# Splitting one tile's attention scores into two sets of four products, in the second layer of a two-layer gated attention and expert kernel

## The chip, the cores and the metric

The kernel runs on one core of a Trainium2 chip. The metric is device time in microseconds (us), the median of several executions. The engines named below are PE (TensorE, matrix products; PEld is its loading of weights), DVE (VectorE), ACT (ScalarE), POOL (GpSimd) and SP (SyncE, which here issues DMAs). Each engine runs its own program in order; they meet by semaphores, counters that one engine raises and another waits for.

## The reference, cut to what matters

Two layers follow each other over x, 64 sequences of 64 rows of 128 numbers. Each layer is a cross attention to a context and then a layer of experts. The part that the change touches is the second layer's attention:

```
q = (query @ qw + qb)   k = (key @ kw + kb)   v = (value @ vw + vb)      # 16 heads of 8
scores = jnp.einsum('bqhd,bkhd->bhqk', q * scale, k)
attn = jax.nn.softmax(scores, axis=-1)
out = jnp.einsum('bhqk,bkhd->bqhd', attn, v)
x = x + jnp.tanh(g_xattn[1]) * (out @ out_proj_weight + out_proj_bias)
```

The second layer has no mask; the first has one. All values are 32-bit floats.

## The kernel before, in words

The 4,096 rows of x are cut into 32 tiles of 128 rows, two sequences each. The attention of both layers is one function, `attention`, called with `of(0)` and `of(1)`; `masked` is true in the first layer alone. Tiles are numbered through both layers: t runs from 0 to 31 in the first and from 32 (`NT`) to 63 in the second. Tiles are gathered in groups of two or four for the projections.

One tile's scores are 128 query rows by 16 heads by 64 keys, which fill four banks of PSUM: `S_ps[0]` holds heads 0 to 7 (half 0) and `S_ps[1]` heads 8 to 15 (half 1). `score` (line 841) writes them with eight products, for each sequence b of the tile and each quarter q of the 128 channels one. A product uses 32 rows and 64 columns of the array, at the place (q * 32, b * S) in it, so that the eight lie on eight different places. Quarters 0 and 1 write half 0, quarters 2 and 3 write half 1. In the trace each product leaves two records, so a tile has 16 (line 852).

DVE then works on each half: `maximum(h)` (line 593) takes the largest score of each row and head, `subtract(h)` (line 601) writes the scores less this maximum into `prob` in SBUF and raises `shifted`. After that the half of PSUM may be written again. PE turns the halves (`turn_probs`, line 863, into `T_ps`), ACT takes the exponential (line 530, into `probT`), and PE multiplies by the values (`attend`, line 878, into `A_ps`). There is one `S_ps` and one `T_ps`, and no second copy of either. POOL lays the keys out in blocks for the products (`k_blk`, line 427), two tiles deep.

Every engine's order is written out by hand: a list of steps, each with its items and a function that gives the time of each item, in iterations of one tile; `run` sorts by that time and, where times are equal, by the place in the list. On PE, `score` of tile t stands first in iteration t - 1, `turn_probs(1)` of tile t - 1 follows it, then `attend` of tile t - 2, the projections, `turn_probs(0)` of tile t, and at the iteration's end `turn_r` and `turn_x` for other groups. On DVE, `maximum(0)`, `subtract(0)`, `maximum(1)` and `subtract(1)` of a tile follow each other, and the smaller work (divisions, statistics, top values, slots) comes after them, ahead of the next tile's `maximum(0)`.

The semaphores that matter: `scored` counts tiles whose eight products are done, and both `maximum(0)` and `maximum(1)` wait for it. `shifted` counts subtractions, two for each tile. `score` of tile t waits for `shifted` of 2t, that is for both subtractions of tile t - 1, and for its queries (`qT_ready`, ACT line 524) and key blocks (`kblk_ready`).

Of the kernel before, what the change touches and what calls it, by code (L numbers as in the profile page):

```python
# [18 lines left out]
NT = B * S // P  # L19
# [19 lines left out]
def wait(eng, sem, value):  # L39

    if not (isinstance(value, int) and value <= 0):
        eng.wait_ge(sem, value)
# [68 lines left out]
GROUP_OF = {t: g for g in GROUPS for t in g.tiles}  # L111
# [20 lines left out]
def shift(skew):  # L132
    return lambda t: t + skew
# [21 lines left out]
def settled(skew, steady, short, later=()):  # L155
    return lambda g: g.last + (steady if g.own < short else lag(g) + skew + (g.own in later))
# [28 lines left out]
def attention(nc, ctx, space, x_all, r_xn, ws, dram, rs, hooks):  # L185
# [13 lines left out]
    def sem(name):  # L199
        return nc.alloc_semaphore(name=name)  # L200
# [65 lines left out]
    qT_ready = sem("qT_ready")  # L266
# [4 lines left out]
    zeroed = sem("zeroed")  # L271
    kblk_ready = sem("kblk_ready")
    scored = sem("scored")
    max_ready = sem("max_ready")
    shifted = sem("shifted")
    probs_turned = sem("probs_turned")
# [37 lines left out]
    def of(layer):  # L314
        w, r, hook = ws[layer], rs[layer], hooks[layer]
        masked = layer == 0
        E = E0 if masked else E1
        short = 3 if masked else LAST_GROUPS
# [270 lines left out]
        def vector(dve):  # L589
            def maximum(h):  # L590
                def step(t):
                    dve.wait_ge(scored, t + 1)
                    nc.vector.tensor_reduce(maxes[:, t % 2, h, :, :], half_of(h), X, ALU.max).then_inc(max_ready, 1)  # L593
                return step

# [171 lines left out]
        def tensor(pe):  # L767
# [59 lines left out]
            def mask_half(h, g, u):  # L827
                for k in range(2):
                    nc.tensor.matmul(S_ps[h][:, k, 0:HQ * S].rearrange("p (e k) -> p e k", k=S), w["ident_bf"][:, :],  # L829
                                     mask_bias[:, g.at(R), u, :].unsqueeze(1).to_broadcast([P, HQ, S]),  # L830
                                     start=True, stop=False, skip_group_check=True)
# [6 lines left out]
                wait(pe, shifted, 2 * t - 1)  # L838
                mask_half(0, g, t - g.first)

            def score(t):
                g = GROUP_OF[t]
                u = t - g.first
                pe.wait_ge(qT_ready, g.i + 1)
                pe.wait_ge(kblk_ready, t + 1)
                wait(pe, shifted, 2 * t)
                if masked:
                    mask_half(1, g, u)
                for b in range(2):
                    for q in range(4):  # L850
                        rows = slice(q * 32, (q + 1) * 32)
                        last = nc.tensor.matmul(S_ps[q // 2][b * S:(b + 1) * S, q % 2, 0:HQ * S], qT[rows, g.at(R), u, b * S:(b + 1) * S],  # L852
                                                k_blk[rows, t % 2, b, :, :], start=not masked, stop=True,
                                                skip_group_check=True, tile_position=(q * 32, b * S))
                last.then_inc(scored, 1)

            def turn_probs(h):
                def step(t):
# [32 lines left out]
            def output(g):  # L891
                pe.wait_ge(r["bias_ready"], 1)
                x_bank.take(y_added, g.i + 1)
                for u in range(g.n):
# [3 lines left out]
            score_ahead = (score, tiles, score_at)  # L898
            awake = [] if masked else [(lambda n: stream_into(T_ps, n), [Q // 2], lambda _, when=when: when) for when in (NT - 3.95, NT - 1.99)]
            awake += [] if masked else [(lambda n: stream_into(T_ps, n), [Q], lambda _: NT - 1)]  # L900
            steps = [score_ahead] + awake + [(turn_probs(1), tiles, shift(0)),
                     (rank if masked else rank_slots, groups, settled(7 if masked else 8, 12, short, later)), (attend, tiles, shift(1)), (logit, groups[:7], settled(6, 9, short, later)),
                     (turn_av, groups, tail(2)), (project_q, groups, head(-2)), (output, groups, tail(3)),
                     (logit, groups[7:], settled(6, 9, short, later)),
                     (project_v, late_units, unit_head(-1)), (project_k, late, head(-3)),
                     (turn_probs(0), tiles, shift(-1)), (mask_first, tiles if masked else [], shift(-2)), (turn_r, groups, settled(5, 8, short, later)), (turn_x, groups, turn_x_at)]
            run(hook["first_tensor"](pe) + steps + hook["tensor"](pe))

        main.tensor, ahead.tensor = tensor, tensor_ahead
# [966 lines left out]
```

## Time and profile before

| | us |
|---|---|
| median of 3 runs (513.63 to 516.26) | 513.66 |
| the profiled execution, whole | 512.48 |
| the profiled execution, span from first to last instruction | 510.7 |
| first layer's attention and experts | to about 280 |
| second layer's attention | about 280 to 428 |
| second layer's experts | from about 428 |

The profile is of one execution. A row of the timeline has the start from the span's beginning and the length in us, then engine, line of the kernel, operation, what is written and read, the shape, and how many instructions are merged in the row; in brackets stands how long the engine had been idle before, and who ended it. A granted clock of 1.00 is 2.4 GHz.

### The profile page before, as it was taken

What the parts mean: (1) busy time and instruction counts of PE and PEld (TensorE: products, weight loads), DVE (VectorE), ACT (ScalarE), POOL (GpSimd) and SP (SyncE); (2) the same over time, 40 slices, a digit from 0 to 9 for tenths busy, and PEclk for the clock granted to TensorE, in tenths of its full rate; (3) what the DMA queues carried; (4) which work ended last, traced back from release to release, by engine and by line L of the source; (5) the groups of instructions that cost most, each with busy time, mean ns of one, the idle gap of its engine ahead of it and who ended that gap; (6) DMA issues with size and microseconds to landing.
All of it is one profiled execution on the core that took longest, in us unless ns stands there. A gap on an engine that the chain in (4) does not pass through costs nothing.

```text
span 510.7 us, 21982 instructions
## 1 busy us (share of the span) xinstructions
PE 438.4 (86%) x8481; PEld 321.1 (63%) x8481; DVE 359.5 (70%) x949; ACT 322.7 (63%) x755; POOL 272.7 (53%) x325
## 2 busy tenths in 40 slices
PE   2788999799978785999998789998999688798986
PEld 1455677567756685999983456666667456554544
DVE  5778879878778765455541788889998787664555
ACT  2555575566766783677754556776778467676663
POOL 2632535545475268888886544544552481544444
PEclk9999999999999998899999899999999899999999
DMA  7225434232110145565436001110031000000112
GB/s 209 51 57 153 98 104 126 70 106 71 46 55 29 35 126 101 78 97 71 45 35 148 14 4 45 46 33 3 25 85 35 23 4 4 3 1 16 43 42 68
DMA packets 50629, 30.69 MB, mean 60 GB/s; under 512 B 12384, under 2 KB 46944, under 8 KB 50528
## 3 DMA queue, kind: packets, MB, share of 16 engines
q1 hardware_dynamic: 37072, 18.54, 13.6%
q0 software_dynamic: 6640, 4.67, 7.0%
q10 hardware_dynamic: 6816, 6.07, 4.2%
q8 instruction: 70, 1.15, 0.9%
q14 instruction: 31, 0.25, 0.2%
HBM read 19.41 MB, written 9.85 MB: 57 GB/s over the span
## 4 chain that ended last, share of the span: by engine, by line
PE 43%; DVE 23%; issue 18%; POOL 7%; ACT 4%; DMA 3%; ACTq 1%; DVEq 1%; POOLq 0%; SPq 0%
DVE maxes L593 8%; PE S_ps L852 6%; PE T_ps L863 5%; POOL x_mid L1145 4%; PE A_ps L878 4%; PE m_H_ps L1478 3%; DVE prob L601 3%; PE S_ps L829 2%; PE m_X_ps L1505 2%; PE Q_ps L825 2%; PE m_T_ps L1518 2%; PE f_H_ps L1197 2%; PE Q_ps L737 2%; PE m_X_ps L1489 2%; PE m_X_ps L1461 2%
## 5 line engine op out<-in xcount | busy, mean ns | idle before, releaser
L593 DVE TENSOR_REDUCE maxes<-S_ps 128x8 f32<-128x512 f32 x128 | 87.6, 685 | 40.5 <-PE S_ps L852 40.5
L427 POOL TENSOR_TENSOR k_blk<-kT,col_a 128x512 f32<-128x512 f32 x64 | 67.7, 1068 | 77.7 <-ACT kT L488 54.5
L530 ACT ACTIVATE probT<-T_ps 128x512 f32<-128x512 f32 x128 | 76.0, 594 | 43.5 <-PE T_ps L863 42.8
L863 PE MATMUL T_ps<-col_a,prob 128*128 128x128 f32 x512 | 83.4, 287 | 9.8 <-DVE prob L601 6.1
L601 DVE TENSOR_TENSOR prob<-S_ps,maxes 128x512 f32<-128x512 f32 x128 | 88.5, 692 | 4.4
L863 PEld LDWEIGHTS T_ps<-col_a,prob 128*128 128x128 f32 x512 | 56.7, 143 | 48.0 <-issue 34.4
L1145 POOL DMA_INDIRECT x_mid<-f_out,f_rows x39 | 60.9, 1562 | 11.9 <-issue 11.9
L852 PE MATMUL S_ps<-k_blk,qT 32*64 32x256 f32 x1024 | 46.5, 415 | 5.0 <-DVE prob L601 4.1
L1010 DVE TENSOR_TENSOR f_hid<-f_H_ps,f_b 128x512 f32<-128x512 f32 x39 | 27.0, 692 | 32.4 <-PE f_Y_ps L1211 27.0
L878 PE MATMUL A_ps<-v_blk,probT 128*32 128x18 f32 x4096 | 48.7, 187 | 0.2 <-issue 0.2
L878 PEld LDWEIGHTS A_ps<-v_blk,probT 128*32 128x32 f32 x4096 | 42.0, 110 | 9.7 <-issue 8.8
L1197 PE MATMUL f_H_ps<-f_rowsT,f_w_now 128*128 128x128 f32 x312 | 42.5, 280 | 4.7 <-ACT f_rowsT L1156 4.7
L1211 PE MATMUL f_Y_ps<-f_w,f_hid 128*128 x312 | 42.6, 281 | 0.7 <-ACT f_hid L1168 0.6
L1197 PEld LDWEIGHTS f_H_ps<-f_rowsT,f_w_now 128*128 128x128 f32 x312 | 39.1, 197 | 4.9 <-ACT f_rowsT L1156 4.9
L464 POOL DMA_INDIRECT sorted_rows<-r_xn,row x32 | 32.1, 1003 | 14.4 <-DVE row L673 7.0
L1211 PEld LDWEIGHTS f_Y_ps<-f_w,f_hid 128*128 128x128 f32 x312 | 38.8, 195 | 1.3 <-issue 1.1
L513 ACT ACTIVATE xn<-x_all,shift_by,rstd 128x128 f32<-128x128 f32 x64 | 31.0, 493 | 10.7 <-DVE shift_by L631 10.7
L497 ACT COPY v_blk<-Q_ps 64x256 f32<-64x256 f32 x64 | 23.9, 373 | 19.4 <-PE Q_ps L748 18.9
L1387 POOL TENSOR_SCALAR m_other<-row_constants,r_slot,r_gap 128x128 f32<-128x128 f32 x32 | 25.4, 800 | 19.7 <-DVE m_combine L1354 19.3
L449 POOL TENSOR_TENSOR x_all<-x_all,row_constants 128x512 f32<-128x512 f32 (+1 forms) x20 | 21.1, 1056 | 25.3 <-ACT xn L513 20.9
L1168 ACT ACTIVATE f_hid<-f_hid 128x512 f32<-128x512 f32 x39 | 24.6, 631 | 15.8 <-DVE f_hid L1010 15.7
L456 POOL TENSOR_SCALAR r_spread<-r_stats 128x4 f32<-128x4 f32 (+1 forms) x20 | 3.9, 194 | 55.5 <-DVE r_stats L642 55.5
(200 smaller groups left out, 867.6 us busy)
## 6 DMA issues: line engine op xcount, KB each, us to landing
f_w<-in_W ACTq DMA_DIRECT2D x16, 256.0 KB, 2.8
ctxT<-in_ctxT SPq DMA_DIRECT2D x12, 256.0 KB, 3.0
f_rows<-sorted_rows SPq DMA_DIRECT2D x39, 64.5 KB, 2.0
out<-m_final SPq DMA_DIRECT2D x32, 64.0 KB, 1.5
x_all<-in_x SPq DMA_DIRECT2D x6, 256.0 KB, 5.8
x_mid<-x_all SPq DMA_DIRECT2D x6, 256.0 KB, 2.5
x_all<-x_mid SPq DMA_DIRECT2D x6, 256.0 KB, 3.6
ctxT<-in_ctxT SPq DMA_DIRECT2D x8, 128.0 KB, 2.6
```

The source lines that it names most:

```text
L427: nc.gpsimd.tensor_tensor(k_blk[:, t % 2, :, :, :], kT[:, g.at(R), t - g.first, :].rearrange("p (b k) -> p b k", b=2).unsqueeze(2).to_broa ...
L464: pool.indirect_dma_start(r["sorted"], bass.IndirectOffsetOnAxis(ap=row[:, t:t + 1], axis=0), r_xn[:, t, :], None).then_inc(scattered[t >= ...
L513: nc.scalar.activation(xn[:, g.at(XR), u, :], x_of(t), ACT.Identity, bias=shift_by[:, g.i % NR, u:u + 1], scale=rstd[:, g.i % NR, u:u + 1] ...
L530: nc.scalar.activation(probT[:, t % 2, 4 * h:4 * h + 4, :], T_ps[:, :, :], ACT.Exp, scale=SCALE).then_inc(probT_ready, 1)
L593: nc.vector.tensor_reduce(maxes[:, t % 2, h, :, :], half_of(h), X, ALU.max).then_inc(max_ready, 1)
L601: nc.vector.tensor_tensor(prob[:, t % 2, heads, :].rearrange("p (r e) k -> p r e k", r=2), half_of(h), maxes[:, t % 2, h, :, :].unsqueeze( ...
L852: last = nc.tensor.matmul(S_ps[q // 2][b * S:(b + 1) * S, q % 2, 0:HQ * S], qT[rows, g.at(R), u, b * S:(b + 1) * S], k_blk[rows, t % 2, b, ...
L863: last = nc.tensor.transpose(T_ps[:, j, :], pair, ident[:, :])
L878: last = nc.tensor.matmul(AV[queries, m + j, :], probT[:, t % 2, j, queries], v_blk[:, g.at(R), t - g.first, c * part // S, j, :], start=T ...
L1145: pool.indirect_dma_start(r["x_mid"], bass.IndirectOffsetOnAxis(ap=rows[:, t % RINGS, D:RW].bitcast(I32), axis=0), out[:, t % DEEP, :], No ...
L1197: last = pe.matmul(H_ps[t % 2][:, n, :], w1_now[:, t % 2, n * P:(n + 1) * P], rowsT[:, t % 2, :], start=True, stop=True)
L1211: last = pe.matmul(Y_ps[t % 2][:, 0:D], hid[:, t % 2, n, :], w2[:, bass.ds(e, 1), n, :].rearrange("p a c -> p (a c)"), start=n == 0, stop= ...
```

## The change

In the second layer the eight products of a tile are made as two sets of four. The first set, quarters 0 and 1 for both sequences, fills half 0 of the scores. It is a step of its own, `score_first`, at the end of the list of iteration t - 2, which is right ahead of `score` of the same tile. It waits for queries, key blocks and `shifted` of 2t - 1, the first subtraction of the tile in front, and raises a new semaphore, `scored_first`. The second set, quarters 2 and 3, fills half 1, waits for `shifted` of 2t as all eight did, and raises `scored`. `maximum(0)` of the second layer waits for `scored_first`, `maximum(1)` still for `scored`. The first layer's products stay one set of eight.

```diff
         def vector(dve):
             def maximum(h):
                 def step(t):
-                    dve.wait_ge(scored, t + 1)
+                    if h == 0 and not masked:
+                        dve.wait_ge(scored_first, t - NT + 1)
+                    else:
+                        dve.wait_ge(scored, t + 1)
...
-            def score(t):
+            def products(t, quarters):
                 g = GROUP_OF[t]
                 u = t - g.first
-                pe.wait_ge(qT_ready, g.i + 1)
-                pe.wait_ge(kblk_ready, t + 1)
-                wait(pe, shifted, 2 * t)
-                if masked:
-                    mask_half(1, g, u)
                 for b in range(2):
-                    for q in range(4):
+                    for q in quarters:
...
-                last.then_inc(scored, 1)
+                return last
+
+            def score_first(t):
+                pe.wait_ge(qT_ready, GROUP_OF[t].i + 1)
+                pe.wait_ge(kblk_ready, t + 1)
+                pe.wait_ge(shifted, 2 * t - 1)
+                products(t, (0, 1)).then_inc(scored_first, 1)
+
+            def score(t):
+                g = GROUP_OF[t]
+                wait(pe, shifted, 2 * t)
+                if masked:
+                    pe.wait_ge(qT_ready, g.i + 1)
+                    pe.wait_ge(kblk_ready, t + 1)
+                    mask_half(1, g, t - g.first)
+                products(t, range(4) if masked else (2, 3)).then_inc(scored, 1)
...
+            split = tiles if not masked else []
+            steps = [(score_first, split[:2], score_at), score_ahead] + awake + [(turn_probs(1), tiles, shift(0)),
...
-                     (turn_probs(0), tiles, shift(-1)), (mask_first, tiles if masked else [], shift(-2)), (turn_r, groups, settled(5, 8, short, later)), (turn_x, groups, turn_x_at)]
+                     (turn_probs(0), tiles, shift(-1)), (mask_first, tiles if masked else [], shift(-2)), (turn_r, groups, settled(5, 8, short, later)), (turn_x, groups, turn_x_at), (score_first, split[2:], shift(-2))]
```

PE's order around the scores of the second layer's tile 13 (t = 45), before. `T_ps` takes the turned probabilities, `X_ps` and `Q_ps` those of other groups; the brackets name the semaphores waited for.

```order
L863 MATMUL T_ps<-col_a,prob 128x128 [waits probT_ready,shifted]
L863 MATMUL T_ps<-col_a,prob 128x128 x3
L788 MATMUL X_ps<-col_a,r_xn 128x128 [waits y_added,r_xn_ready]
L788 MATMUL X_ps<-col_a,r_xn 128x128
L852 MATMUL S_ps<-k_blk,qT 64x256 [waits shifted,kblk_ready,qT_ready]
L852 MATMUL S_ps<-k_blk,qT 64x256 x7
L863 MATMUL T_ps<-col_a,prob 128x128 [waits probT_ready,shifted]
```

The same place after the change, where lines have moved (852 is 851 now, 863 is 877, 788 is 792):

```order
L877 MATMUL T_ps<-col_a,prob 128x128 [waits probT_ready,shifted]
L877 MATMUL T_ps<-col_a,prob 128x128 x3
L792 MATMUL X_ps<-col_a,r_xn 128x128 [waits y_added,r_xn_ready]
L792 MATMUL X_ps<-col_a,r_xn 128x128
L851 MATMUL S_ps<-k_blk,qT 64x256 [waits shifted,kblk_ready,qT_ready]
L851 MATMUL S_ps<-k_blk,qT 64x256 x3
L851 MATMUL S_ps<-k_blk,qT 64x256 [waits shifted]
L851 MATMUL S_ps<-k_blk,qT 64x256 x3
L877 MATMUL T_ps<-col_a,prob 128x128 [waits probT_ready,shifted]
```

No instruction of another kind has changed its place: both sets stand where the eight products stood, and a wait stands between them. On DVE the same tile's work reads, before:

```order
L593 TENSOR_REDUCE maxes<-S_ps 128x8 [waits scored]
L601 TENSOR_TENSOR prob<-S_ps,maxes 128x512 [waits probs_turned,max_ready]
L593 TENSOR_REDUCE maxes<-S_ps 128x8 [waits scored]
L601 TENSOR_TENSOR prob<-S_ps,maxes 128x512 [waits probs_turned,max_ready]
L609 RECIPROCAL rden<-A_ps 128x32 [waits av_made]
```

and after the change:

```order
L597 TENSOR_REDUCE maxes<-S_ps 128x8 [waits scored_first]
L605 TENSOR_TENSOR prob<-S_ps,maxes 128x512 [waits probs_turned,max_ready]
L597 TENSOR_REDUCE maxes<-S_ps 128x8 [waits scored]
L605 TENSOR_TENSOR prob<-S_ps,maxes 128x512 [waits probs_turned,max_ready]
L613 RECIPROCAL rden<-A_ps 128x32 [waits av_made]
```

The order is the same; the first maximum of a tile has another semaphore to wait for.

## Rows read from the trace of the kernel before

**Rows 1.** The page: span, and busy time of each engine.

```profile
span 510.7 us, 21982 instructions
PE 438.4 (86%) x8481; PEld 321.1 (63%) x8481; DVE 359.5 (70%) x949; ACT 322.7 (63%) x755; POOL 272.7 (53%) x325
```

**Rows 2.** Windows over 280 to 428: their sum and mean of 20 us.

```profile
sum 148.00, PE 127.75 PEld 89.87 DVE 125.38 ACT 97.62 POOL 69.03; mean PE 18.25 PEld 12.84 DVE 17.91 ACT 13.95 POOL 9.86
```

**Rows 3.** Waits from 280 to 428: us in all, times, longest.

```profile
DVE maxes L593 <- PE S_ps L852: 16.8, 21, 3.0
PE S_ps L852 <- DVE prob L601: 4.1, 8, 0.8
PE T_ps L863 <- ACT probT L530: 2.3, 11, 0.3
```

**Rows 4.** Timeline around tile 13: PE reaches the scores ahead of DVE.

```profile
333.75 0.69 DVE L601 TENSOR_TENSOR prob<-S_ps,maxes 128x512 f32<-128x512 f32 x1
334.06 0.38 PE L788 MATMUL X_ps<-col_a,r_xn 128*128 128x128 f32 x2
334.55 0.27 PEld L852 LDWEIGHTS S_ps<-k_blk,qT 32*64 32x64 f32 x16 [0.35 <-issue]
334.58 0.69 PE L852 MATMUL S_ps<-k_blk,qT 32*64 32x256 f32 x16
335.37 0.69 DVE L593 TENSOR_REDUCE maxes<-S_ps 128x8 f32<-128x512 f32 x1 [0.59 <-PE S_ps L852]
```

**Rows 5.** Timeline around tile 11: PE reaches the scores behind DVE.

```profile
326.30 0.23 PEld L852 LDWEIGHTS S_ps<-k_blk,qT 32*64 32x64 f32 x16 [0.17 <-issue]
327.09 0.69 DVE L593 TENSOR_REDUCE maxes<-S_ps 128x8 f32<-128x512 f32 x1 [0.82 <-PE S_ps L852]
```

**Rows 6.** Pieces of the chain that ended last, 280 to 428: start, us, what.

```profile
290.86 0.76 PE S_ps L852 x16
...
291.65 0.70 DVE maxes L593
...
307.35 0.62 PE S_ps L852 x16
...
421.89 0.70 PE S_ps L852 x16
...
422.62 0.70 DVE maxes L593
```

**Rows 7.** Timeline around tiles 2, 5, 21 and 27: scores and the maximum behind them.

```profile
290.83 0.27 PEld L852 LDWEIGHTS S_ps<-k_blk,qT 32*64 32x64 f32 x16 [0.29 <-issue]
291.65 0.69 DVE L593 TENSOR_REDUCE maxes<-S_ps 128x8 f32<-128x512 f32 x1 [0.59 <-PE S_ps L852]
...
301.96 0.27 PEld L852 LDWEIGHTS S_ps<-k_blk,qT 32*64 32x64 f32 x16 [0.35 <-issue]
302.78 0.69 DVE L593 TENSOR_REDUCE maxes<-S_ps 128x8 f32<-128x512 f32 x1 [0.93 <-PE S_ps L852]
...
371.58 0.27 PEld L852 LDWEIGHTS S_ps<-k_blk,qT 32*64 32x64 f32 x16 [0.53 <-issue]
372.40 0.69 DVE L593 TENSOR_REDUCE maxes<-S_ps 128x8 f32<-128x512 f32 x1 [0.60 <-PE S_ps L852]
...
398.35 0.27 PEld L852 LDWEIGHTS S_ps<-k_blk,qT 32*64 32x64 f32 x16 [0.97 <-issue]
399.16 0.69 DVE L593 TENSOR_REDUCE maxes<-S_ps 128x8 f32<-128x512 f32 x1 [0.17 <-PE S_ps L852]
```

**Rows 8.** Timeline at 395: one product of 256 columns, and its reader.

```profile
395.18 0.60 PE L737 MATMUL Q_ps<-ctxT,col 128*128 128x256 f32 x2
...
395.86 0.48 ACT L488 ACTIVATE kT<-Q_ps,col 128x256 f32<-128x256 f32 x1
```

**Rows 9.** Windows, line 852, tile 13: stretch, length, PE (instructions), PEld (instructions), clock, DMA.

```profile
334.50:334.70 0.20, 0.12 (x8) 0.15 (x16) 1.00 0.00 0
334.70:334.95 0.25, 0.25 (x16) 0.12 (x15) 1.00 0.00 0
```

More of the change, by code:

```diff
@@ L273, in attention @@
     scored = sem("scored")
+    scored_first = sem("scored_first")
     max_ready = sem("max_ready")
@@ L900, in tensor @@
             awake += [] if masked else [(lambda n: stream_into(T_ps, n), [Q], lambda _: NT - 1)]
-            steps = [score_ahead] + awake + [(turn_probs(1), tiles, shift(0)),
+            split = tiles if not masked else []
+            steps = [(score_first, split[:2], score_at), score_ahead] + awake + [(turn_probs(1), tiles, shift(0)),
                      (rank if masked else rank_slots, groups, settled(7 if masked else 8, 12, short, later)), (attend, tiles, shift(1)), (logit, groups[:7], settled(6, 9, short, later)),
```

## The prediction

> **What bounds the kernel now.** The change touches the second layer's attention alone, so I read that stretch, 280 to 428, and not the page's shares [rows 1], which mix it with the first layer and the experts. The windows come first: of its 148 us PE is busy 127.75 and DVE 125.38, the other engines far less [rows 2]. No single engine is the bound; two nearly full engines hand one tile's scores to and fro. The list of waits says where: DVE's longest wait is for the scores, 16.8 us in 21 pieces, and in the other direction PE waits 4.1 us in 8 pieces, ahead of the scores, for DVE's subtraction [rows 3].
>
> Then the timeline. At tile 13 [rows 4] DVE ends its second subtraction at 334.44 (333.75 + 0.69). PE's last work before the scores begins at 334.06, and then its weight loading stands idle for 0.35 us: it waits for that subtraction. The products begin at 334.58, and the next maximum at 335.37, 0.79 us later. DVE has filled a part of this with smaller work and waits 0.59 us. Tile 11 is the other kind [rows 5]: its weight loading is idle for only 0.17 us, which is what going over to these products costs with nothing to wait for, and DVE waits 0.82 us because PE is late. The change can start work earlier at a tile of the first kind alone.
>
> Last, the chain that ended last tells what a wait is worth. Between 280 and 428 it goes from a tile's scores to the maximum behind them 11 times, first at 290.86 and last at 421.89 [rows 6]. Other waits for scores lie beside the chain: there PE's own row of products, or DVE's smaller work, is as long, and shortening them moves nothing. At five of the 11 PE was ahead of DVE: 290.86, 301.99, 334.58, 371.62 and 398.38. At the other six it came late or waited for queries, which the first set waits for too.
>
> **The change, part by part.** Nothing is added in products or DVE work, and no instruction changes its place on any engine; a wait and a semaphore's raise stand between the two sets.
>
> *The first set's earlier start.* It waits only for the first subtraction of the tile in front, which `turn_probs(0)`, just ahead of it, has waited for already. So it starts when PE arrives. How much earlier that is, I take from the idle time of the weight loading less the 0.17 us of a late tile [rows 5]: 0.29 - 0.17 = 0.12 at tile 2, 0.18 at tile 5, 0.36 at tile 21, 0.80 at tile 27 [rows 7], 0.18 at tile 13 [rows 4]. DVE can use no more than it waits: 0.59, 0.93, 0.60, 0.17 and 0.59 us. The lesser of the two is 0.12 + 0.18 + 0.36 + 0.17 + 0.18 = 1.01 us. Gains at waits beside the chain I count as nothing. The cover is what makes them worthless: PE's products and DVE's small work run on without a pause there. If that cover went, each would be worth as much as those counted, so the whole 2.88 us of DVE's five waits is the bound above for this term (PE arrives earlier too once DVE has run ahead), and nothing the bound below.
>
> *A set of four against one of eight.* The first maximum starts when four products are done instead of eight. How long four take, no row shows. The bound above is eight: 0.79 us from the first product to the maximum [rows 4]. The bound below is a single product of the same 256 columns, whose reader starts 395.86 - 395.18 = 0.68 us after it [rows 8]; this is an estimate, since the reader is ACT. So the gain lies between 0 and 0.11 us. I take 0.04, nearer to eight, since the eight run beside each other: eight records start by 334.70 and all 16 by 334.95 [rows 9], and both of a product's records have to pass in a set of four as well. At the chain's 11 passages this gives 11 x 0.04 = 0.44 us, with bounds of 0 and 1.21.
>
> A rule of the Trainium skill prices the same thing from the other end ("TensorE: Matmul & The Clock Gate", Part 3, "The cost: per-tile semaphore tail"): the tail behind tiled products grows by 4.7 ns for each tile. Four tiles fewer would be 0.02 us, an estimate from that page, and the sum would be 0.22 us less than mine.
>
> *The second set.* It waits for the second subtraction as all eight did. Where PE is early it starts when the eight started; where PE is late it stands right behind the first set with its wait already met. I cost it at nothing: the products lie on eight places of the array, and PE has all 16 weight loads started by 334.70 [rows 9]. DVE does not meet it, as it needs half 1 only after a maximum and a subtraction, 0.69 us each [rows 4]. Behind the waiting set on PE stand `turn_probs(1)` of the tile in front, `attend` and the projections; they waited behind the eight in the same way. The cost if the two sets do not run beside each other is the third rival.
>
> *The extra wait and raise.* A tile's scores begin with no more idle time than 0.17 us though they wait for three semaphores [rows 5], so a met wait shows no cost of its own. I take 0; the bound above is 0.02 us for each of the 32 tiles, as between the end of the scores at 291.62 (290.86 + 0.76) and the maximum at 291.65 in the chain [rows 6], 0.6 us in all.
>
> *Sum.* 1.01 + 0.44 = 1.45 us less. The profiled execution took 512.48 us, 1.8 more than its span [rows 1], and becomes 511.0. The median of the runs, 513.66, is 1.2 us above the profiled one; the change does not touch that difference, so the forecast is 513.66 - 1.45 = **512.2 us**. With the bounds: 513.66 - 2.88 - 1.21 = 509.6 and 513.66 + 0.6 = 514.3.
>
> **What is late next.** At tiles where DVE no longer waits, PE's own row of products sets the pace, with `turn_probs(1)` behind `T_ps`: PE waits there for ACT's exponential, 2.3 us in 11 pieces [rows 3]. DVE running ahead does not free `T_ps` sooner.
>
> **The rivals.**
>
> 1. *Nothing arrives at the end.* DVE's time goes into another wait: PE is busy 127.75 of 148 us as its pipelined ends are drawn [rows 2], and the wait of `turn_probs(1)` for ACT stays [rows 3]. For it: only 4.1 us of PE's time in the whole stretch is spent on the wait that the change relaxes. Against it: the five passages are on the chain. The time would be from 0.8 us below the present to 0.5 above, 512.9 to 514.2, around 513.5.
>
> 2. *DVE gets all its waits back.* Once DVE is ahead, the subtractions come earlier, PE starts earlier in turn, and the five waits of the chain vanish whole, with sets of four as short as one product: 2.88 + 1.21 = 4.1 us, 509.6. Half of the way beyond my sum is 2.8 us, 510.9. For it: DVE's waits of 0.59 to 0.93 us are larger than PE's spare time that I counted. Against it: six of the 11 passages have PE late, where only the smaller set helps.
>
> 3. *Slower: the second set runs behind the first.* Of a tile's 16 records eight start between 334.58 and 334.70, and the other eight between 334.70 and 334.95 [rows 4, 9]: two waves, the second 0.12 to 0.37 us behind the first. If the waves are a rule of order, so that nothing of the second set starts before the first set's second wave has, late scores take a wave or two more, some 0.25 us (the middle of the two). The chain runs from PE's earlier work into late scores nine times, first at 307.35 and last at 421.89 [rows 6]: 9 x 0.25 = 2.25 us more, against 1.01 us of gain at early tiles, gives 514.9. If it costs that at all 24 of the 32 tiles at which no wait for the subtraction is listed (8 pieces, [rows 3]), it is 6.0 us more and 518.6. It decides from 0.11 us for a late tile, where nine times that eats the gain. For it: the first set takes quarters 0 and 1 for both sequences, so its third product lies on the same rows as its first, where the eight ran through four quarters before they came back to one. Against it: all 16 weight loads had started by 334.70, among them those of products on rows that were still busy.
>
> A rule of the Trainium skill stands behind this rival ("TensorE: Matmul & The Clock Gate", Part 3, "The mechanism"): products start and end strictly in program order, and a weight load overlaps a running product only when its row group differs. By it the new order within a set would lose overlap, and the time would be that of this rival, 514.9 to 518.6. This case's trace does not bear out its second half, as 16 loads [rows 9] start while the first products of the same rows are under way.
>
> **How the numbers follow.** The forecast, 0.8 to 2.5 us less, gets 0.54; nothing at the end 0.22; all waits back 0.14; the second set behind the first 0.10. The predicted time is that of the first. The range, 510.2 to 515.4, takes in the first two cases, half of the third and the cheapest of the fourth. A change of 0.5%, 2.6 us, is about what a measurement of this kernel can tell from none. Faster by more needs 511.1 or less: the third case and the tail of the first, 0.19. Slower by more needs 516.2 or more: the dearer part of the third rival and a little for what I don't see, 0.08. The rest, 0.73, is within.
>
> **What the changed profile would show.** DVE's wait for scores should fall from 16.8 us to about 12, by more than the kernel gains, since waits beside the chain fall too. At early tiles the first records of the scores should stand right behind `turn_x`, `turn_r` or `turn_probs(0)` and ahead of the subtraction's end, and the maximum right behind DVE's smaller work. At late tiles the 16 records should still begin within 0.3 us or so; if they spread over 0.5 us or more, the third rival holds. From a set's first product to its maximum should lie about 0.75 us. I would be wrong if PE's idle time moves to `T_ps` in full, if late scores grow, or if the experts' stage behind 428 changes its length.

## The result, and the profile after

The changed kernel takes 508.97 us in the median of 20 runs (504.47 to 514.95), the kernel before 513.66 us beside it: a ratio of 0.9896, 95% interval 0.9872 to 0.9920. The medians differ by 4.7 us; the ratio leaves out the runs more than 1.5% above the fastest of their kernel (three of the changed, two of the one before), and by it the change takes 5.3 us or 1.04%, where 1.45 us were forecast. The time is outside the range given, which began at 510.2. In a second measurement the ratio was 0.9916. The profiled execution took 508.26 us, 4.22 us less than that of before.

The page of the changed kernel, with the span and the busy times, answers to [rows 1]:

```profile
span 506.5 us, 21982 instructions
PE 441.6 (87%) x8481; PEld 322.8 (64%) x8481; DVE 359.2 (71%) x949; ACT 323.1 (64%) x755; POOL 273.0 (54%) x325
```

Its windows over 280 to 428, and its waits in that stretch, answer to [rows 2, 3]:

```profile
sum 148.00, PE 131.96 PEld 93.05 DVE 126.54 ACT 100.10 POOL 69.43; mean PE 131.96 PEld 93.05 DVE 126.54 ACT 100.10 POOL 69.43
```

```profile
DVE maxes L597 <- PE S_ps L851: 14.2, 15, 2.5
...
PE T_ps L877 <- DVE prob L605: 5.0, 4, 2.9
...
PE T_ps L877 <- ACT probT L531: 2.5, 11, 0.4
...
PEld S_ps L851 <- DVE prob L605: 2.1, 4, 0.5
```

DVE's wait for scores fell from 16.8 us in 21 pieces to 14.2 in 15, by less than the forecast fall to about 12. PE's wait for the subtraction ahead of the scores is no longer among its own rows. The wait for ACT's exponential stayed (2.3 before, 2.5 now).

The timeline around tile 13, PE and DVE's maximum, answers to [rows 4]:

```profile
331.80 0.69 DVE L605 TENSOR_TENSOR prob<-S_ps,maxes 128x512 f32<-128x512 f32 x1
...
332.12 0.38 PE L792 MATMUL X_ps<-col_a,r_xn 128*128 128x128 f32 x2
...
332.43 0.33 PEld L851 LDWEIGHTS S_ps<-k_blk,qT 32*64 32x64 f32 x16 [0.17 <-issue]
332.43 0.78 PE L851 MATMUL S_ps<-k_blk,qT 32*64 32x256 f32 x16
...
333.16 0.69 DVE L597 TENSOR_REDUCE maxes<-S_ps 128x8 f32<-128x512 f32 x1 [0.32 <-PE S_ps L851]
```

The first set starts at 332.43, ahead of the end of the second subtraction (331.80 + 0.69 = 332.49), with the bare 0.17 us of going over in place of 0.35. The maximum follows 0.73 us behind the first product (0.79 before), and DVE waits 0.32 us in place of 0.59. This is what the prediction described.

Where the 4.22 us between the two profiled executions lie, by the starts of the scores in each trace (tiles are counted from 0 in each layer):

| stretch | before, us | changed, us | difference |
|---|---|---|---|
| start to tile 2 of the first layer | 25.41 | 27.02 | +1.61 |
| first layer, tiles 2 to 31 | 142.00 | 137.86 | -4.14 |
| to tile 1 of the second layer (experts between) | 119.32 | 119.42 | +0.10 |
| tiles 1 to 2 of the second layer | 4.14 | 5.11 | +0.97 |
| second layer, tiles 2 to 31 | 130.96 | 128.17 | -2.79 |
| the rest (second experts) | 88.85 | 88.88 | +0.03 |

The first and fourth rows vary as much between two traces of the changed kernel (27.02 and 25.34, 5.11 and 3.76 us), so I read nothing out of them. The surprise is the second row: the first layer's eight products were not split, and this stretch lost more than the second layer's.

Its place is found in PE's timeline. The kernel before, on its router's products and what follows:

```profile
96.70 0.74 PE L878 MATMUL A_ps<-v_blk,probT 128*32 128x18 f32 x64
97.30 0.42 PE L798 MATMUL X_ps<-col_b,r_xnT 128*32 128x8 f32 x29
99.66 0.23 PE L798 MATMUL X_ps<-col_b,r_xnT 128*32 128x8 f32 x3 [1.94 <-issue]
...
102.56 1.16 PE L852 MATMUL S_ps<-k_blk,qT 32*64 32x256 f32 x16
```

The same instructions of the changed kernel:

```profile
97.90 0.74 PE L892 MATMUL A_ps<-v_blk,probT 128*32 128x18 f32 x64
98.50 0.55 PE L802 MATMUL X_ps<-col_b,r_xnT 128*32 128x8 f32 x32
...
101.05 0.69 PE L851 MATMUL S_ps<-k_blk,qT 32*64 32x256 f32 x16
```

Before, 29 of 32 equal products run, PE stands still for 1.94 us with no semaphore to wait for ("issue"), and three follow. Windows of the kernel before show the pause and what follows it (the last three columns are the granted clock, the DMA share and GB/s):

```profile
97.70:99.60 1.90, 0.02 (x1) 0.00 (x0) 1.83 (x5) 0.00 (x0) 1.81 (x2) 1.00 0.11 35
...
101.00:103.00 2.00, 2.00 (x17) 1.41 (x23) 0.00 (x0) 1.67 (x4) 1.57 (x2) 0.54 0.66 193
103.00:105.00 2.00, 2.00 (x60) 1.06 (x46) 1.14 (x2) 0.46 (x2) 0.00 (x0) 0.61 0.76 211
```

PE had been idle, and between 101 and 105 us it runs at 0.54 and 0.61, near the lower of its two levels (1.2 of 2.4 GHz): 16 records of scores take 1.16 us in place of 0.69. In the changed kernel the clock is 1.00 there. Two more traces, of `before_again` and `layer2_order`, have a pause of 2.2 us at this place, and both have 3.4 us at the low clock behind it. From tile 17 to tile 19 of the first layer the kernel before needs 7.07 + 5.09 us, the changed one 4.36 + 4.20: 3.60 of the 4.14 us. The second layer has a pause of the same kind at 356.12 (1.18 us, the same line) in the kernel before; from the scores of that tile to the next it takes 5.25 us against 4.03 in the changed kernel.

### The profile page after: what moved, and what is told of

Its sections match the earlier page's. It is cut to its first block, busy times and chain, and to the rows that moved or that the text cites. A ratio compares the mean times of both kernels' runs of the same rounds, so it can differ in the third digit from the quotient of the medians.

```text
span 506.5 us, 21982 instructions
## 1 busy us (share of the span) xinstructions
PE 441.6 (87%) x8481; PEld 322.8 (64%) x8481; DVE 359.2 (71%) x949; ACT 323.1 (64%) x755; POOL 273.0 (54%) x325
## 3 DMA queue, kind: packets, MB, share of 16 engines
q8 instruction: 70, 1.15, 0.9%
## 4 chain that ended last, share of the span: by engine, by line
PE 46%; DVE 20%; issue 17%; ACT 6%; POOL 5%; DMA 4%; ACTq 1%; DVEq 1%; SPq 0%; POOLq 0%
DVE maxes L597 7%; PE T_ps L877 7%; PE S_ps L851 5%; PE A_ps L892 4%; PE m_H_ps L1493 3%; PE S_ps L833 2%; PE Q_ps L752 2%; POOL x_mid L1160 2%; DVE prob L605 2%; PE Q_ps L829 2%; PE m_X_ps L1520 2%; PE f_H_ps L1212 2%; PE m_T_ps L1533 2%; PE Q_ps L741 2%; DMA x_mid<-f_out,f_rows 2%
## 5 line engine op out<-in xcount | busy, mean ns | idle before, releaser
L851 PE MATMUL S_ps<-k_blk,qT 32*64 32x256 f32 x1024 | 50.0, 414 | 0.9 <-ACT qT L525 0.3
```

## The experiments

My first theories: A, the whole gain comes from the second layer's split; B, the split gives about the 1.5 us forecast, and the rest comes from the new order in which the first layer's waits are stated, a side of the diff that I had not priced (`shifted` ahead of queries and keys in `score`); C, the first measurement was lucky. All ratios are to the kernel before, run beside.

**The change again, and its parts left out.** `unsplit` has no sets and no `scored_first`, but the new order of waits in both layers:

```diff
                 wait(pe, shifted, 2 * t)
-                if masked:
-                    pe.wait_ge(qT_ready, g.i + 1)
-                    pe.wait_ge(kblk_ready, t + 1)
+                pe.wait_ge(qT_ready, g.i + 1)
+                pe.wait_ge(kblk_ready, t + 1)
...
-            split = tiles if not masked else []
+            split = []
```

`both_sub` keeps the sets, and the first one waits for both subtractions:

```diff
-                pe.wait_ge(shifted, 2 * t - 1)
+                pe.wait_ge(shifted, 2 * t)
```

`whole_max` keeps sets and early start, and `maximum(0)` waits for all eight:

```diff
-                    if h == 0 and not masked:
-                        dve.wait_ge(scored_first, t - NT + 1)
-                    else:
-                        dve.wait_ge(scored, t + 1)
+                    dve.wait_ge(scored, t + 1)
```

> The changed kernel itself, once more, timed beside the kernel before on one chip. Theory A (the gain comes from the second layer alone: DVE no longer waits where PE was ahead, and it adds up over more tiles than the five on the chain): ratio 0.988 to 0.992, and from the first tile's scores to the last tile's in the second layer 3 us or more are missing against the kernel before, apart from PE's stalls that no semaphore ends. Theory B (about 1.5 us comes from there, and the rest from elsewhere: the first layer, whose waits ahead of the scores stand in another order, or how the instructions lie): the same ratio, but only 1 to 2 us of it within the second layer's attention. Theory C (the first measurement was lucky and the gain is 1.5 us): ratio 0.996 to 0.998.

> The eight products are one set again and both maxima wait for all eight; of the change only the new order of the waits ahead of the scores is left, in both layers. Theory A: no difference from the kernel before, ratio 0.998 to 1.002. Theory B: the part of the gain that does not come from the split, ratio 0.992 to 0.996. Theory C: 0.998 to 1.002.

> Two sets with their own semaphores as in the change, but the first set too waits for both subtractions of the tile in front; what is left is the smaller set ahead of the first maximum. Theory A: the early start is the gain, so this gives the small term alone, 0.04 us at each tile that waits: ratio 0.998 to 1.000. A rival to it, that a set of four frees DVE much sooner than one of eight: ratio below 0.995, and from the first product to the maximum 0.70 us or less instead of 0.79.

> The first set starts early as in the change, but the first maximum waits for all eight products as before. DVE gains nothing from the early start, PE only by the shorter second set. Theory A: ratio 0.998 to 1.000, since the gain is DVE's. A rival to it, that the gain is PE's (less work behind the second subtraction): ratio 0.990 to 0.994, near the whole gain.

| kernel | ratio | 95% interval |
|---|---|---|
| again | 0.9916 | 0.9885 to 0.9947 |
| unsplit | 0.9936 | 0.9897 to 0.9975 |
| both_sub | 0.9964 | 0.9929 to 1.0000 |
| whole_max | 0.9942 | 0.9909 to 0.9975 |

C falls: the gain is there again. A is in trouble: without any split 0.6% are gained. `both_sub` and `whole_max` lie between the two ratios that their expectations name. The intervals overlap, so the traces have to tell the parts, and there they are sharp. Call the time from the end of one tile's second subtraction to the end of the next tile's the period of that next tile. In the second layer many tiles have one and the same period, which comes back to 0.02 us in other traces of a kernel where no pause falls into it (us, worked out from the records of the traces):

| tile | before | unsplit | both_sub | whole_max | changed |
|---|---|---|---|---|---|
| 5 | 3.67 | 3.59 | 3.60 | 3.52 | 3.47 |
| 9 | 3.67 | 3.59 | 3.60 | 3.52 | 3.30 |
| 13 | 3.67 | 3.59 | 3.61 | 3.52 | 3.40 |
| 17 | 3.67 | 3.59 | 3.60 | 3.52 | 3.30 |
| 21 | 3.67 | 3.59 | 3.60 | 3.53 | 3.23 |
| 27 | 3.67 | 3.59 | 3.60 | 3.52 | 3.41 |

A set of four alone is worth 0.06 to 0.07 us (`both_sub`), the order of waits alone 0.08 (`unsplit`). The second set's single wait together with its being of four gives 0.15 where DVE waits for that set (`whole_max`), and the early start, with DVE on the first set, 0.05 to 0.29 more. Shorter than before are ten tiles, 3, 5, 7, 9, 13, 17, 19, 21, 23 and 27, not five.

**The order of waits in one layer alone.** `layer1_order` is the kernel before with this edit for the first layer only, `layer2_order` with it for the second only; `split_old_order` is the change without it:

```diff
+                wait(pe, shifted, 2 * t)
                 pe.wait_ge(qT_ready, g.i + 1)
                 pe.wait_ge(kblk_ready, t + 1)
-                wait(pe, shifted, 2 * t)
```

`turn_order` is the change with the waits of `turn_probs(1)` exchanged, `probT_ready` first.

> The kernel before, with one thing of the change: in the first layer the scores wait for the second subtraction first and for queries and key blocks after it. The second layer is as it was. Theory B (a wait's place in the list sets how soon PE answers): in the first layer the product after the wait starts 0.06 us after the subtraction instead of 0.15, in the second still 0.15; ratio 0.994 to 0.998, and from the third tile's scores to the last in the first layer 138 to 139 us. Theory A (all from the split): 0.15 in both, ratio 0.998 to 1.002.

> The change without its new order of waits in the first layer: the split alone. Theory B: the split's own part, 2.2 us of the second layer's attention as in the traces so far, ratio 0.994 to 0.997, and 0.15 us again in the first layer. Theory A: nearly the whole gain, ratio 0.988 to 0.992.

> The kernel before, with the new order of waits in the second layer alone and no split. Theory B: 0.06 us after the subtraction in the second layer, 0.15 in the first; about 0.9 us less from the second layer's third tile to its last (128.9 apart from PE's stalls that no semaphore ends); ratio 0.997 to 0.999. Theory A: ratio 0.998 to 1.002 and no change of the 0.15.

> The change, and the same reordering at another wait: the second half's turning waits for the exponential first and for the subtraction, long done, last. Theory B: PE answers the exponential some 0.08 us sooner, at 11 places in the second layer's attention and about as many in the first; 1 to 2 us less than the change, ratio 0.986 to 0.990. If the order matters at the scores alone (a change of the array's layout stands there and not here): no difference from the change, 0.990 to 0.992.

| kernel | ratio | 95% interval |
|---|---|---|
| layer1_order | 0.9979 | 0.9940 to 1.0018 |
| split_old_order | 0.9944 | 0.9904 to 0.9985 |
| layer2_order | 0.9968 | 0.9933 to 1.0003 |
| turn_order | 0.9872 | 0.9837 to 0.9907 |

Each part gives about what B says, none beyond doubt. What the order does is seen where PE waits for the subtraction. In the kernel before that subtraction starts at 94.34 and lasts 0.69 us; PE and then DVE:

```profile
95.18 0.38 PE L829 MATMUL S_ps<-mask_bias,ident_bf 128*128 128x256 bf16 x2
...
94.34 0.69 DVE L601 TENSOR_TENSOR prob<-S_ps,maxes 128x512 f32<-128x512 f32 x1
```

In the changed kernel, the same tile:

```profile
96.37 0.39 PE L833 MATMUL S_ps<-mask_bias,ident_bf 128*128 128x256 bf16 x2
...
95.62 0.69 DVE L605 TENSOR_TENSOR prob<-S_ps,maxes 128x512 f32<-128x512 f32 x1
```

95.18 is 0.15 us behind the subtraction's end, 96.37 is 0.06. It is so at each tile of the first layer where the products start as soon as the subtraction lets them.

**Is it a met wait at the end, or the place of the late one?** `met_last` says the wait for keys once more behind the subtraction's; two kernels are repeated to narrow them, and the kernel before is run against itself.

```diff
                 wait(pe, shifted, 2 * t)
+                pe.wait_ge(kblk_ready, t + 1)
```

> The kernel before once more, as a zero point for the ratios and as another trace of it. Expected 0.998 to 1.002. If the stalls without a releaser near 99 and 356 us belong to the order of waits in the first layer and in the second, stalls of 0.3 to 2 us are there again at the same lines, and the first layer's stretch is again near 141.5 to 142 us; if they were an accident of one trace, the stretch is near 139.5 us.

> The kernel before, with the wait for the keys, already met, said once more behind the wait for the second subtraction, in both layers; no scores are split. If TensorE answers faster because the last wait ahead of the products is one already met, the gap from the end of the second subtraction to the next product is 0.05 to 0.06 us in place of 0.15 in both layers, and the ratio is that of the kernel with the new order of waits and no split, about 0.994. If it is the place of the wait for the subtraction, first of the three, that counts, the gap stays 0.15 us and the ratio is 1.000.

> Once more the kernel before with the new order of waits in the first layer alone, to narrow its ratio. Theory B (the order of waits gives about half): 0.995 to 0.997. Theory A (all from the second layer's split): 1.000.

> Once more the change with the old order of waits in the first layer, to narrow its ratio. Theory B: 0.994 to 0.996, some 0.004 above the whole change. Theory A: 0.990, as the whole change.

| kernel | ratio | 95% interval |
|---|---|---|
| before_again | 0.9981 | 0.9947 to 1.0015 |
| met_last | 0.9990 | 0.9964 to 1.0017 |
| layer1_again | 0.9962 | 0.9930 to 0.9993 |
| split_again | 0.9870 | 0.9826 to 0.9914 |

The answer of `met_last` fits neither of its two expectations. The same tile in its trace, PE and DVE:

```profile
97.55 0.38 PE L829 MATMUL S_ps<-mask_bias,ident_bf 128*128 128x256 bf16 x2 [0.17 <-issue]
...
96.61 0.69 DVE L601 TENSOR_TENSOR prob<-S_ps,maxes 128x512 f32<-128x512 f32 x1
```

The product starts 0.25 us behind the subtraction. The records of PE's semaphore instructions tell why. In the compiled program the first of several waits that are stated ahead of a product stands on the product's own weight load, and the others on separate semaphore instructions ahead of it, two to an instruction. Tile 15 of the first layer, us behind the end of the subtraction:

| kernel | semaphore instructions that begin | weight load | product |
|---|---|---|---|
| before: queries, keys, `shifted` | 0.04 | 0.12 | 0.15 |
| met_last: queries, keys, `shifted`, keys | 0.04 and 0.15 | 0.22 | 0.25 |
| changed: `shifted`, queries, keys | none | 0.05 | 0.06 |

Each semaphore instruction that stands between the late wait and the product costs 0.1 us. The Trainium skill ("Perfetto Trace Analysis", "Identifying Dependency Chains") says that instructions that wait for several engines may have such instructions put ahead of them; the trace agrees, and adds the 0.1 us each.

Still `met_last` costs no time that can be measured, though ten tiles of the first layer and eleven of the second answer 0.1 us later, and `split_again`, with the old order, measures 0.9870, which neither theory had, where the same kernel gave 0.9944 before. The two intervals still overlap, and the two traces took the same time (508.99 and 509.01 us), so no trace shows what lies between these measurements. `before_again` pauses near 99 us again, and its first layer's stretch is again long, 142.27 us. What varies most from trace to trace are the pauses. I counted the place of each among all of PE's instructions, in order of their records, for pauses over 0.3 us without a semaphore (the table leaves out one of 0.35 us among the experts):

```
kernel           end of pause, us (length)     place
before           99.66 (1.94)  356.12 (1.18)   14*256+193  50*256+193
before_again     99.66 (2.23)  327.62 (1.11)   14*256+193  44*256+193
                 357.69 (1.18) 410.94 (0.59)   50*256+193  60*256+194
met_last         101.28 (1.25) 122.72 (0.81)   14*256+194  18*256+193
                 377.79 (1.14) 427.24 (0.71)   54*256+193  63*256+193
changed          404.19 (0.59)                 60*256+194
```

In 20 traces there are 48 such pauses, and 40 of them, all above 0.42 us among them, stand at place 256 n + 193 or 194. The page of every kernel has a queue of instructions, with packets, MB and share; this is the row of the changed one:

```profile
q8 instruction: 70, 1.15, 0.9%
```

1.15 MB in 70 packets is 16 KB each, and PE's 17,948 records in 70 parts are 256 each: a packet holds 256 of PE's instructions. In front of the end of the pause, at 99.66, a packet of this queue begins at 97.44 and takes 0.97 us; in the changed kernel it begins at 96.46, and PE does not stop. All 20 traces together let PE pass such a place 1,380 times. It never does so sooner than 2.16 us behind the start of the packet that belongs to the block in front, and after each pause over 0.42 us at such a place it goes on 2.2 to 2.9 us behind it (2.22 us at 99.66). So the pauses are PE waiting for its own instructions. The Trainium skill ("Runtime: NRT & Kernel Launch", "Instruction fetch mechanics") gives blocks of 256 instructions, and says that the cost of going from one to the next is mostly hidden. The blocks agree; here up to 2.2 us are not hidden.

**Moving the packets alone.** Theory D: most of the gain beyond the forecast is that packets fell elsewhere. These kernels have waits already met ahead of PE's first product, which waits until 7.58 us anyway: 32 or 56 instructions more on PE's queue, and nothing else. `late_first` is `turn_order` with the order of waits changed at seven more places.

```diff
         @block.tensor
         def _(pe):
+            for _ in range(64):
+                pe.wait_ge(consts, 2)
             first.tensor(pe)
```

> The kernel before with 64 waits at TensorE's start, all met by 1 us, ahead of its first product (which waits until 7.58 us): 32 more instructions on its queue, nothing else moved. In the traces so far every stall without a releaser stands at place 256 n + 193 of TensorE's instructions, beside a 16 KB packet of the instruction queue. If the stalls come from instructions that arrive late, they move by 32 places, to other lines than L798 at 99.66 us and 356.12 us, some go or come, and the time lies anywhere between 0.992 and 1.004 with the first layer's stretch of 142.0 us changed by more than 0.5 us. If they belong to the order of waits, L798 still stalls by 1.9 and 1.2 us and the ratio is 0.999 to 1.002.

> The same with 112 waits, 56 more instructions, for a second distance (the last of them may end near the 7.58 us at which the first product is released, up to 0.3 us lost at the start). Late instructions: stalls at places 256 n + 193 again, 56 instructions earlier in the program than without, and a time between 0.992 and 1.005. Order of waits: as the kernel before.

> The changed kernel with the same 32 instructions ahead. If about 0.7% of the gain of 1.04% lies in where instruction packets happen to land, the ratio to before moves away from 0.990 with the stalls in its trace, up to 0.996 if there are stalls of 3 us in all; the first layer's waits still answer in 0.06 us and the second layer's stretch without stalls is 127.6 us as in the change. If the gain is in the split and the order of waits alone, the ratio stays 0.989 to 0.992.

> The change with, at eight places on TensorE, the wait that is met last stated first, so that it stands on the product itself and not on an instruction ahead of it (the first set's scores, the first mask, second turn of probabilities, keys, turns of x and of the router's rows, the second experts' moves and hidden products). By the trace 40 to 50 of these places wait, at 0.08 us each: the products begin 0 to 0.06 us after the release in place of 0.08 more; where half of it reaches the end, 1.5 to 2 us: 0.985 to 0.988, if no stall of another place takes it back. If the order of waits gives nothing that arrives, 0.988 to 0.991 as the change and its other orders.

> The changed kernel with 56 instructions ahead, beside the kernel before at the same distance (0.9916). If the change alone is worth what the periods of undisturbed tiles show (1.9 us in the second layer, 0.5 us in the first: 0.46%), it is 0.984 to 0.990 here; if the change is worth nothing beyond where packets fall, 0.991 to 0.993. The periods of tiles 9, 17, 19 and 21 of the second layer are 3.30, 3.30, 3.28 and 3.23 us again, against 3.67 us.

> The kernel with the last-met waits first at eight places (0.9847) with 32 instructions ahead. If its gain over the change is in the order of waits, 0.983 to 0.988; if it was where its packets fell, 0.988 to 0.992.

| instructions ahead | before | changed | late_first |
|---|---|---|---|
| none | 0.9981 (0.9947 to 1.0015) | 0.9896 (0.9872 to 0.9920) | 0.9847 (0.9810 to 0.9883) |
| 32 | 0.9929 (0.9900 to 0.9957) | 0.9875 (0.9828 to 0.9922) | 0.9847 (0.9799 to 0.9895) |
| 56 | 0.9916 (0.9879 to 0.9954) | 0.9824 (0.9787 to 0.9861) | |

The rows with idle instructions are also ratios to the kernel before without any. The kernel before becomes 0.7 to 0.8% faster by instructions that do nothing. Its two pauses, at 99.66 and 356.12, are gone, and others stand at the same places of other blocks. One of them, in `before_pad56`, between two products of line 829:

```profile
63.43 0.27 PE L829 MATMUL S_ps<-mask_bias,ident_bf 128*128 128x256 bf16 x1
64.90 0.28 PE L829 MATMUL S_ps<-mask_bias,ident_bf 128*128 128x256 bf16 x1 [1.19 <-issue]
```

That is place 7 * 256 + 194. The first layer's stretch is 139.62 us there in spite of it, against 142.00. That fewer pauses make the 0.8% isn't shown by this trace as a whole, though: its pauses at such places come to 4.9 us, against 3.1 in the kernel before, and it took 512.26 us, against 512.48. At the same number of instructions ahead the changed kernel lies below the one before by 1.04 and 0.84% (none, two measurements), 0.54% (32) and 0.93% (56), the last two uncertain by some 0.5%, and its undisturbed periods are the same with all three (tile 9: 3.30, 3.30, 3.30). The expectation of 0.984 to 0.990 at 56 was narrowly missed on the fast side. So was that of the kernel before at 56, and `change_pad32` and `late_first` also lie a little below what either theory gave them.

`late_first` holds 0.9847 at two distances, below both kernels of this case at the same distances; against the changed one the intervals overlap, so what the eight places add isn't settled. Its second experts' stretch is not shorter (89.6 against 88.9 us), though two of the eight places lie there.

## Why the prediction was wrong

**The step that failed** is the sum, which put "1.01 + 0.44 = 1.45 us less" on the median of before and took all else as unchanged, on the ground that "no instruction changes its place on any engine" and that "a met wait shows no cost of its own". In the second layer 2.4 us arrive where the two terms gave 1.45. The wait term, put at 0, is a gain of 0.5 us in the first layer alone. And the order of products was unchanged, but the time and the form of the waits were not: the kernel before has pauses in it, 3.60 us with what follows at one of them, that an edit elsewhere can move.

*Early start and set of four*, 1.01 + 0.44 us: the right mechanism, too small. By the least period of each tile over four traces of a kernel, tiles 3 to 27 of the second layer take 106.43 us before and 104.01 in the change, 2.4 us less (what the waits give there is in it). The set of four is worth 0.06 us a tile, where I took 0.04: 0.73 us to the maximum in place of 0.79. The Trainium skill's 4.7 ns a tile ("TensorE: Matmul & The Clock Gate", Part 3, "The cost: per-tile semaphore tail") gave 0.02; the measurement decides against it here.

The early start reaches ten tiles and not five. I counted only the passages of the chain from scores to the maximum (11 by my count; the chain has 10). At tiles 3, 9, 17 and 23 it goes another way, from the subtraction through the scores to `turn_probs(1)`. At tile 9 of the kernel before:

```profile
317.81 0.70 DVE prob L601
318.51 0.14 issue
318.65 0.69 PE S_ps L852 x16
319.34 0.60 PE T_ps L863 x4
```

There PE itself is held up by the subtraction and has eight products to make behind it; after the change it has four. These four tiles and the counted 5, 13, 21 and 27 are eight of the ten. The other two, 7 and 19, lay beside the chain of that execution; by their period, 3.67 us where no pause disturbs it, the same circle of subtraction, scores and maximum bound them. Part of the gain is given back at the tiles behind: tile 3 gains 0.69 us and tile 4 loses 0.50, tile 9 gains 0.37 and tile 10 loses 0.24. So the 2.4 us lie between my 1.45 and the 4.1 of the second rival, which holds in part.

*The extra wait and raise*, taken as 0 with 0.02 a tile as a bound: the sign was wrong. The second set's single wait answers 0.1 us sooner than the three waits did. In the first layer, which I did not price at all, the new order takes 0.08 us off tiles 2, 5, 7, 9, 13, 17 and 21 (3.99 to 3.91 us at tile 9), and with small gains and losses at others 0.47 us in all.

*Not in the prediction*: PE's pauses for its instructions, 3.60 us with the low clock in the first layer and 1.18 us in the second, in the pair of profiled executions. Of the second some 0.85 us arrive: from the tile of the pause over three tiles the scores take 13.97 us, and 13.12 in `before_pad56`, which has no pause there. At 32 and 56 idle instructions the kernel before has no pause at these two places, with its waits as they were, so the pauses don't belong to the waits as such. Without idle instructions they do go with the order of waits: of these traces, all six with the old order in the first layer pause at block 14, by 0.67 to 2.23 us, and of the nine with the new order eight have none over 0.3 us there and one has 0.34. So it is no accident of one execution: where the new order moves PE's work by a little, this pause is gone. The prediction's chain of waits was followed from semaphore to semaphore, and such a pause, which the trace shows as "issue", has none.

*The rivals.* The first, that nothing arrives, falls. The third, that the second set runs behind the first, falls too: at a late tile all 16 records still start within 0.31 us (0 to 47 ns and 266 to 314 ns after the first), and where the second set comes later, its first wave starts ahead of the first set's second (tile 9: 0 to 20 and 266 to 286 ns, against 223 to 243 and 490 to 510).

So 2.4 + 0.5 = 2.9 us, 0.56%, is the change's own by the undisturbed periods, and the measured 0.54 to 1.04% at equal distances agree with it or lie above. That the rest of the first measurement is pauses is argued and not measured: 2.9 us and the 3.60 us of one pause are already more than the 5.3 measured, and how often the executions without a trace pause isn't known.

*What stays open.* Why a packet comes late. In the kernel before it begins 3.6 us behind the place 193 of the block in front, as a load of 256 KB on the scalar queue ends; in the changed kernel 1.4 us behind it, ahead of that load (the median of all packets is 1.2). That would fit a queue behind the load, but at 356 us a packet begins 3.1 us behind its place with no load in sight. No run tries it.

## What to carry to other kernels

State the wait that is met last as the first one ahead of a product: it then stands on the product's weight load, and the met ones pass ahead of it. Before an edit is priced at under 1%, look for pauses without a releaser in the kernel before, and compare versions with a few idle instructions ahead of each: here 32 or 56 of them, which move the places of the instruction packets, were worth 0.7 to 0.8%, as much as the edit. A wait beside the chain can be worth something all the same: tiles whose periods agree to 0.01 us can be bound by one circle, and what shortens it then counts at each of them.

## What the runs showed of the hardware

PE stops for 0.3 to 2.2 us at place 193 or 194 of a block of 256 of its instructions when a 16 KB packet of them is late: in 1,380 cases it never passed this place sooner than 2.16 us behind the packet's start. After the pause of 1.94 us its clock was at about half, from 101 to 105 us (0.54 and 0.61). A separate semaphore instruction on PE costs 0.1 us (0.06, 0.15 and 0.25 us with none, one and two behind the release). Products of two sets on eight places of the array do not pass strictly one behind the other: a later set's first wave of records starts between the two waves of the set in front (tile 9: from 223 ns, and the second wave in front from 266 ns).
